# Attention taken head by head: projections between the scores, row sums in fours, norms in packs of four

## The reference

```python
x = x + 0.5 * ffn(layernorm(x))                  # gelu, 1024 -> 4096 -> 1024, weights changed per sequence
xn = x1 / max(|x1|, 1e-12) * sqrt(1024) * gamma  # x1 = layernorm(x)
q, k, v = split(xn @ w_qkv.T)                    # 8 heads of 128
sim = (q * 128 ** -0.5) @ k.T                    # causal mask, per head
out = softmax(sim) @ v                           # 2048 x 2048 per head
x = x + out @ w_out.T
x = x + 0.5 * ffn(layernorm(x))
```

## Time and profile before

| | us |
|---|---|
| median of 3 runs | 2884.86 |
| lowest of them | 2884.67 |
| profiled execution | 2884.55 |
| its span on the slowest core (core 3) | 2883.0 |
| spans of all cores | 2873.4 to 2883.0 |
| PE busy | 2762.4 (96%) |
| DVE busy | 1535.2 (53%) |
| ACT busy | 1173.1 (41%) |
| first attention, first projection to first output projection | 524.4 to 926.5 |

### The profile page before, as it was taken

One profiled execution on the slowest core, in us unless ns is written; L12 is line 12 of the kernel. 1 busy time (PEld: TensorE's weight loads), 2 busy tenths in 40 slices (PEclk: granted clock), 3 DMA queues, 4 the chain that ended last, 5 costly groups with the idle time before them and its releaser, 6 DMA issues.

```text
span 2883.0 us, 39821 instructions; the slowest of 8 cores (2873.4 to 2883.0 us)
## 1 busy us (share of the span) xinstructions
PE 2762.4 (96%) x12944; PEld 1259.0 (44%) x12944; DVE 1535.2 (53%) x2060; ACT 1173.1 (41%) x1901; POOL 34.5 (1%) x61
## 2 busy tenths in 40 slices
PE   4999999999999999999999999999999899999999
PEld 1444444444444444444444444444444443444444
DVE  6457447546346744744753663565452557456343
ACT  3331332468677233233223223226775852321320
POOL 0000000000000000000000000000000000000000
PEclk9999999999999999999999999999999999999999
DMA  5634433220020144653574354350301103446433
GB/s 164 219 118 145 165 124 129 37 45 1 1 59 1 59 159 138 214 190 139 192 224 147 114 157 155 116 111 7 45 1 23 37 1 112 151 151 200 147 132 132
DMA packets 57905, 321.55 MB, mean 112 GB/s; under 512 B 6384, under 2 KB 6512, under 8 KB 24944
## 3 DMA queue, kind: packets, MB, share of 16 engines
q1 hardware_dynamic: 43504, 281.26, 29.2%
q0 software_dynamic: 14208, 37.75, 6.4%
HBM read 318.99 MB, written 16.78 MB: 116 GB/s over the span
## 4 chain that ended last, share of the span: by engine, by line
PE 92%; DVE 4%; issue 2%; DMA 1%; ACT 1%; SPq 0%; DVEq 0%; ACTq 0%
PE ps L392 31%; PE ps L376 29%; PE ps L432 7%; PE ps L477 4%; PE ps L469 4%; PE ps L435 4%; PE ps L457 4%; PE ps L491 4%; PE ps L334 1%; PE ps L311 1%; DVE tB L852 1%; DVE wb L751 1%; PE ps L444 1%; PE ps L301 1%; DMA xn<-wall 1%
## 5 line engine op out<-in xcount | busy, mean ns | idle before, releaser
L751 DVE SCALAR_TENSOR_TENSOR wb<-ps,oddc,xn 128x512 bf16<-128x512 f32 x1024 | 692.0, 743 | 489.5 <-PE ps L334 439.2
L376 PE MATMUL ps<-xn,wb 128*128 128x512 bf16 x4096 | 911.6, 383 | 25.9 <-DVE xn L729 14.0
L392 PE MATMUL ps<-arena,wb 128*128 128x512 bf16 x4096 | 907.3, 379 | 0.0
L376 PEld LDWEIGHTS ps<-xn,wb 128*128 128x128 bf16 x4096 | 403.5, 99 | 526.0 <-issue 55.6
L392 PEld LDWEIGHTS ps<-arena,wb 128*128 128x128 bf16 x4096 | 401.2, 98 | 498.6 <-issue 24.1
L591 ACT ACTIVATE arena<-ps,small 128x512 bf16<-128x512 f32 x512 | 351.8, 687 | 575.8 <-PE ps L376 575.7
L665 ACT ACTIVATE pb<-ps,negm 128x512 bf16<-128x512 f32 (+3 forms) x640 | 353.5, 637 | 57.1 <-PE ps L460 31.8
L599 ACT ACTIVATE pb<-ps,b2half 128x512 f32<-128x512 f32 x128 | 88.0, 687 | 662.2 <-PE ps L392 662.2
L799 DVE TENSOR_TENSOR R<-R,pb 128x512 f32<-128x512 f32 x128 | 88.6, 692 | 378.6 <-ACT pb L599 378.4
L469 PE MATMUL ps<-pb,onesb 128*128 128x512 bf16 (+3 forms) x640 | 224.4, 356 | 29.9 <-DVE tB L852 17.2
L432 PE MATMUL ps<-xn,wb 128*128 128x512 bf16 x1024 | 237.9, 379 | 0.0
(11 more groups left out here) (61 smaller groups left out, 1307.1 us busy)
## 6 DMA issues: line engine op xcount, KB each, us to landing
xn<-wall SPq DMA_DIRECT2D x256, 1024.0 KB, 5.9
wb<-wall POOLq DMA_DIRECT2D x16, 1024.0 KB, 10.6
outT<-R POOLq DMA_DIRECT2D x24, 512.0 KB, 4.7
R<-xT SPq DMA_DIRECT2D x16, 512.0 KB, 9.0
R<-xT POOLq DMA_DIRECT2D x16, 512.0 KB, 7.4
outT<-R SPq DMA_DIRECT2D x16, 256.0 KB, 6.0
meanf<-mean_f SPq DMA_DIRECT2D x1, 64.0 KB, 8.9
meanb<-mean_bf SPq DMA_DIRECT2D x1, 32.0 KB, 9.5
```

The costliest lines, as they stand in the source:

```text
L376: m = pe.matmul(ps[i][:, :], wt[:, cc * 512 + i * 128: cc * 512 + (i + 1) * 128], xsl(st, cc, t0 + nh * 512), start=(cc == 0), stop=(cc == ...
L392: m = pe.matmul(ps[b][:, :], wt[:, k * 128:(k + 1) * 128], h_act(k // 4 + 8 * (k % 4), nh), start=(k == 0), stop=(k == HC - 1))
L751: i = dve.scalar_tensor_tensor(wb[n % 3][:, cc * 512:(cc + 1) * 512], ps[4][:, :], odd[:, i0 * 8 + cc: i0 * 8 + cc + 1], F[half][:, k * 51 ...
```

## The change

- One list, `SCHED`, holds the whole attention of a sequence. `FIRST` projects heads 0 and 1 of Q and K and the V of heads 0 to 3 ahead of the scores. The other 64 groups (`LATER`) are taken in half groups, eight matmuls each, between the score tiles: after each product with V as many as the rate gives, one half group for two tiles (128 half groups over the first 256 of 320 tiles). They and the norms use banks 6 and 7 by turns.
- A group of V now gives 256 tokens by two heads: two times eight matmuls of 256 columns. V is evicted by DVE, Q and K still by ACT.
- Scores use three banks (0, 1, 2), outputs banks 3 and 4 by turns, the row sums bank 5 alone. The sums of four tiles run in a row after the fourth product with V (`sum`); pb has eight slots.
- The norms of one head's four blocks of Q (or K) are made by four matmuls in a row, each against 32 columns of ones, each writing its own 32 partitions of one bank, followed by one maximum on DVE over the bank. `bound` joins the four maxima by a mask and one f32 matmul of 8 columns; `root` takes the square root by Ln and Exp; `shift` writes the head's own column of negm. For heads 0 and 1 the four squares of Q (K) are made after the fourth block, for the others after each block.
- The sums, squares, mean and variance of the norm of block 1024, and the sum of block 1536, go from the attention into the last two W2 groups of f1. The squares of block 1536 are taken by PE before groups 1 to 4 of the attention and made by ACT after groups 0 to 3.
- The slabs of attention are loaded in the order V, Q, K. K is held for three heads, V for four, in a ring.

The diff, cut to its core (PE's part, then ACT's, then DVE's; the old loops that the new ones replace are printed above):

```diff
-KT0, V0, QT0 = 0, HPH * S, 2 * HPH * S
+QO0, K0, V0, NSQ0 = 0, HEADS * S, HEADS * S + 3 * S, HEADS * S + 3 * S + 4 * S
...
-PROJ = []
-for _nbs in ((0, 1), (2,), (3,)):
-    for _kind in ("q", "k"):
-        for _h in range(HPH):
-            for _nb in _nbs:
-                PROJ.append((_kind, _h, _nb))
...
...
+FIRST = [("q", h, nb) for h in range(2) for nb in range(2)] + [("v", p, t) for p in range(2) for t in range(4)]
+FIRST += [("k", h, nb) for h in range(2) for nb in range(2)]
+FIRST += [("q", 0, 2), ("q", 1, 2), ("v", 0, 4), ("v", 0, 5), ("v", 1, 4), ("v", 1, 5), ("k", 0, 2), ("k", 1, 2)]
+FIRST += [("q", 0, 3), ("k", 0, 3), ("v", 0, 6), ("v", 0, 7), ("v", 1, 6), ("v", 1, 7), ("q", 1, 3), ("k", 1, 3)]
+LATER = []
+for _h in range(2, HEADS):
+    _kinds = [("q", _h, nb) for nb in range(4)], [("k", _h, nb) for nb in range(4)]
+    if _h in (4, 6):
+        LATER += _kinds[0] if _h == 4 else []
+        LATER += [("v", _h // 2, t) for t in range(4)]
+        LATER += _kinds[1] if _h == 4 else _kinds[0] + _kinds[1]
+        LATER += [("v", _h // 2, t) for t in range(4, 8)]
+    else:
+        LATER += _kinds[0] + _kinds[1]
+def with_norms(groups, waiting):
+    out = []
+    for kind, h, nb in groups:
+        for half in range(2):
+            out.append(("proj", kind, h, nb, half))
+            for item in [i for n, i in waiting if n == 0]:
+                out.append(item)
+            waiting[:] = [(n - 1, i) for n, i in waiting if n > 0]
+        if kind == "v":
+            continue
+        if h >= 2:
+            out.append(("sq", kind, h, nb))
+        elif nb == 3:
+            out.extend(("sq", kind, h, i) for i in range(4))
+        if nb == 3:
+            waiting.append((1, ("norm", kind, h)))
+            if kind == "k":
+                waiting.extend([(3, ("bound", h)), (5, ("root", h)), (7, ("shift", h))])
+    return out
+def attn_schedule():
+    waiting = []
+    sched = with_norms(FIRST, waiting)
+    later = with_norms(LATER, waiting)
+    later += [i for n, i in waiting]
+    cost = [1 if i[0] == "proj" else 0 for i in later]
+    total, core = sum(cost), 0
+    done, pending, pre, g = 0, [], {}, 0
...
+        for st in steps:
+            sched.append(st)
+            if st[0] == "pv":
+                if st[3] % 4 == 3:
+                    sched.append(("sum", st[1], st[2], st[3] // 4, st[4], ui))
+                core += 1
+                while later and done <= total * core / (RATE * 40):
+                    item = later.pop(0)
+                    done += item[0] == "proj"
+                    sched.append(item)
+    assert not later
+    return sched
+RATE = 6.4
+SCHED = attn_schedule()
+S_BANK = (0, 1, 2)
+SUM_OF = {i[4]: (i[5], i[3] // 4) for i in SCHED if i[0] == "pv"}
+LAST_G = {i[5]: i[4] for i in SCHED if i[0] == "pv"}
...
-        pb = sb("pb", [128, 2048], BF16)
+        pb = sb("pb", [128, 4096], BF16)
...
+                if n == 15 and st == "f1" and ti == 1:
+                    ln_square("at", seq, 1024, 2 * t)
+                    ln_square("at", seq, 1024, 2 * t + 1)
+                    if t == 3:
+                        ln_mean("at", seq, 1024)
...
+                    if what == "proj" or what == "norm" or what == "bound":
+                        rot = (6, 7) if scoring else (0, 1, 2)
+                        b = rot[turn % len(rot)]
+                    if what == "proj":
+                        _, kind, h, nb, half = item
+                        if half == 0:
+                            if 1 <= groups < 5:
+                                ln_square("at", seq, 1536, 2 * (groups - 1))
+                                ln_square("at", seq, 1536, 2 * (groups - 1) + 1)
+                            if groups == 5:
                                 ln_mean("at", seq, 1536)
+                            groups += 1
+                            bank_free(b)
+                            wt = attn_slab(pe, ("at", seq, h // (2 if kind == "v" else 4), "qkv".index(kind)))
+                            pe.wait_ge(g["xnd"].sem,
+                                       g["xnd"].at(("at", seq, (nb // 2 if kind == "v" else nb) * 512, CC - 1)))
+                        if kind == "v":
+                            for cc in range(CC):
+                                m = pe.matmul(ps[b][:, half * 256:(half + 1) * 256],
+                                              xsl("at", cc, nb * 256 + half * 128, 128),
+                                              wt[:, cc * 512 + (h % 2) * 256: cc * 512 + (h % 2 + 1) * 256],
+                                              start=(cc == 0), stop=(cc == CC - 1))
+                        else:
+                            for cc in range(4 * half, 4 * half + 4):
+                                c0 = cc * 512 + (h % 4) * 128
+                                m = pe.matmul(ps[b][:, :], wt[:, c0:c0 + 128], xsl("at", cc, nb * 512),
+                                              start=(cc == 0), stop=(cc == CC - 1))
+                        if half == 1:
+                            m.then_inc(g["proj_mm"].sem, g["proj_mm"].up((seq, kind, h, nb)))
+                            freed[b] = ("v_ev" if kind == "v" else "proj_ev", (seq, kind, h, nb))
+                            turn += 1
+                    elif what == "norm":
+                        _, kind, h = item
                         bank_free(b)
+                        pe.wait_ge(g["nsq"].sem, g["nsq"].at((seq, kind, h, 3)))
+                        for j in range(4):
+                            m = pe.matmul(ps[b][32 * j:32 * j + 32, :], onesb[:, 0:32],
+                                          arena[:, NSQ0 + j * 512: NSQ0 + (j + 1) * 512], start=True, stop=True)
+                        m.then_inc(g["nrm_mm"].sem, g["nrm_mm"].up((seq, kind, h)))
+                        freed[b] = ("nmax", (seq, kind, h))
+                        turn += 1
+                    elif what == "bound":
+                        h = item[1]
+                        bank_free(b)
+                        pe.wait_ge(g["nmask"].sem, g["nmask"].at((seq, "k", h)))
+                        pe.matmul(ps[b][:, 0:8], meanf[:, :], nrd[:, :], start=True, stop=True).then_inc(
+                            g["bnd_mm"].sem, g["bnd_mm"].up((seq, h)))
+                        freed[b] = ("nprod", (seq, h, 0))
+                        turn += 1
...
+                        b = S_BANK[gi % 3]
+                        bank_free(b)
...
+                        ob, p0 = 3 + ui % 2, (gi % 8) * 512
...
+                    elif what == "sum":
+                        _, h, qb, batch, gi, ui = item
+                        if batch == 0:
+                            bank_free(5)
+                        for j in range(4):
+                            kt = 4 * batch + j
+                            w0 = 128 * max(0, kt - 4 * qb)
+                            p0 = ((gi - 3 + j) % 8) * 512
+                            m = pe.matmul(ps[5][:, w0:512], onesb[:, :], pb[:, p0 + w0:p0 + 512], start=(kt == 0),
+                                          stop=(kt == 4 * qb + 3))
+                        m.then_inc(g["rs_mm"].sem, g["rs_mm"].up((seq, ui, batch)))
+                        freed[5] = ("recip", (seq, ui))
...
+                        if n == 14 and a[0] == "at":
+                            ln_squares("at", seq, 1024)
+                        if n == 15 and a[0] == "at":
+                            ln_musq("at", seq, 1024)
+                            ln_rstd("at", seq, 1024)
...
+                        if groups < 4:
+                            ln_squares("at", seq, 1536, 2 * groups, 2 * groups + 2)
+                        if groups == 6:
+                            ln_musq("at", seq, 1536)
+                        if groups == 9:
+                            ln_rstd("at", seq, 1536)
+                        groups += 1
+                    elif what == "sq":
+                        _, kind, h, nb = item
+                        act.wait_ge(g["proj_ev"].sem, g["proj_ev"].at((seq, kind, h, nb)))
+                        if nb == 0 and held.get("nsq"):
+                            act.wait_ge(g["nrm_mm"].sem, g["nrm_mm"].at(held["nsq"]))
+                        c0 = qcol(h, nb) if kind == "q" else kcol(h, nb * 512)
+                        act.activation(arena[:, NSQ0 + nb * 512: NSQ0 + (nb + 1) * 512], arena[:, c0:c0 + 512],
+                                       AF.Square).then_inc(g["nsq"].sem, g["nsq"].up((seq, kind, h, nb)))
+                        if nb == 3:
+                            held["nsq"] = (seq, kind, h)
...
+                    elif what == "root":
+                        h = item[1]
+                        act.wait_ge(g["nprod"].sem, g["nprod"].at((seq, h, 1)))
+                        act.activation(nrx[:, 3:4], nrx[:, 2:3], AF.Ln, scale=float(DM * DM), bias=cols[:, 1:2]).then_inc(
...
+                        act.activation(nrx[:, 3:4], nrx[:, 3:4], AF.Exp, scale=0.5).then_inc(
```

(59 more changed lines are left out.)

306 lines of the change are left out of this document (115 added, 191 removed).

## The result

The changed kernel takes **2929.57 us** (median of its runs, lowest 2928.05), the kernel before 2884.86 (lowest 2884.67). The ratio is 1.015, with an interval of 1.012 to 1.018: about 45 us slower, under the 2% line. The profiled execution took 2929.54 us with a span of 2928.0, against 2884.55 and 2883.0. The forecast was +60, just over the 2% line; the sign was right and the range held the result, but the size was missed by 15 us.

What follows compares the result with a forecast made beforehand. PE, busy 96%, was taken as the bound. Waits and slow clock of 69.4 us per attention against 35 gave +69, norms -13, bounds and V +4.5: +60 on 2884.55, 2945 us; range 2892 to 2985.

Steps and rivals of the forecast that it cites:

- part 5: Slow clock per attention: seven half-clock stretches, 1.7 us each, four in the scores; 12 us, bounds 5 and 20.
- DVE terms: Between a unit's last sums and its reciprocal: norms 5.6 us, V evictions, bounds and shifts; 8.1 us per attention.
- score banks: In the scores, three banks instead of four: exponentials 0.1 us late after narrow scores, some 16 times; 1.5 us per attention.
- part 4: In the scores: DVE work ahead of the reciprocal 8.1 us, head 7 3.0, three score banks 1.5, per attention.
- head 7's bound and masks: At head 7, PE waits for the square and DVE's mask, and the exponentials for the root; 3.0 us per attention.
- Part 1: Seam from the first feed-forward: PE waits on squares, 1.1 us in W2, 7.8, and 5.5 over three groups; 14.4 per attention.
- Part 2: End of the first projections: PE waits for squares of heads 0 and 1 and the first exponential; 6.8 us per attention.
- Part 3: Row sums in bank 5 alone: waits on reciprocals, 12.6 us while projections last and 11.0 after, per attention.
- the 60 that the prediction gave as a sign of being right: Row-sum matmuls, all in bank 5, were to wait on reciprocals for 60 us or more in sum.
- below 94%: Whole kernel: PE's busy share was to fall below 94%, as a sign that the forecast was right.
- The first rival of the prediction: While projections last, other work covers the row sums' wait at each unit's first batch; 2898 us; chance 0.18.
- Part 6: Norms in 32 packs of four matmuls at 0.45 us each: 13 us won, range -20 to +11.

Runs made afterwards that it cites:

- e10: Changed kernel with block 1024's variance ahead of block 1536's adds, and PE taking 1536's squares two groups later; undisturbed cores 2896.1 to 2898.3 us.
- e5: Changed kernel with row-sum copy before the reciprocal, the seam's other order, and ACT instead of DVE evicting V; lowest 2853.53 us, ratio to before 0.990.
- e4: Changed kernel plus eight 512-column matmuls ahead of the first row sums of each attention's last five units; undisturbed cores 2919.8 to 2923.3 us.
- e8: Kernel before the change, with DVE copying the row sums out of their bank ahead of the reciprocal; lowest 2904.84 us, ratio to before 1.007.
- e11: Changed kernel with only DVE's copy of the row sums out of bank 5 ahead of the reciprocal; undisturbed cores 4 to 7 2895.4 to 2905.1 us.
- e3: Changed kernel with both the row-sum copy ahead of the reciprocal and the seam's other order; lowest 2880.11 us, ratio to before 0.992.

## Why the prediction missed the size, and what in it was right

The places of the waits and the sign were right; the size was 15 us too high, which put the forecast over the 2% line (0.48 was given to that side) and the result under it. The step that failed is part 5, the clock: it put 12 us of slow clock into each attention where there were 6.6, and so forecast 3.5 us more than before where none were added. Smaller shares of the miss are the DVE terms and the score banks of part 4. For each attention the length is set against the prediction's own count of issue, 368.4, less 6.9 for the packs and 2.6 for what moved into W2, plus 2.2 for bounds and V's halves: 361.1. The lengths of the two attentions on core 0, 419.6 and 426.0 us, leave 58.5 and 64.9 of gaps and slow clock, 61.7 in the mean, and 62.9 with the excess of the wait in W2 (1.2). The forecast had 69.4. By steps, means of both attentions:

| step | forecast | measured |
|---|---|---|
| 1 seam | 14.4 | 14.4 |
| 2 end of the first projections | 6.8 | 6.8 |
| 3, 4 row sums, and DVE work ahead of the reciprocal | 31.7 | 29.2 |
| 4 head 7's bound and masks | 3.0 | 1.9 |
| 4 three banks for scores | 1.5 | 0 seen |
| 5 clock | 12 | 6.6 |
| other gaps, most under 0.3 us | none | 4.0 |

- **Part 1 was right** in every link: 7.47 on the square against 7.8 with the second square, three waits of 1.36 against 1.8 less the 0.43 that always pass, 0.83 in W2 against 1.1. e10 took them away and got their time back.
- **Part 2 was right**: 3.7 on norms (L514) and 3.1 on the first exponentials, table loads 16 as said.
- **Part 3 was right** in its place and kind: all waits in bank 5, 0.2 to 0.6 in most units with projections, 1.85 to 2.25 without. As the profile counts waits they sum to 40.9 us in both attentions, not to the 60 that the prediction gave as a sign of being right (the table counts from issue to issue and takes in V's half groups, 58). PE busy came out at 94.5% and not below 94%. The first rival of the prediction, a covered wait, would have had none while projections last.
- **Part 4 was mis-sized**, by about a third of its DVE terms (29.2 less part 3's 23.6 leaves 5.6 of 8.1): the 0.9 for a norm put before the tail was forecast six times in an attention and shows at three places (672.61, 850.20, 886.46); elsewhere the waits are 0.2 to 0.7, and part of the delay appears as V's half groups waiting for their bank (4.7 in both). Head 7's cluster is 1.9, and three score banks cost nothing that shows: of the 4.4 us of L541 3.5 are the first scores of the two attentions, which part 2 has, and 0.9 belong to head 7's cluster.
- **Part 5, the clock, was the step that failed.** Its price of 1.7 for a stretch over busy PE was right, its count and its places were not. It put seven stretches at half clock into each attention, four of them within the scores. The trace of core 0 has four stretches of 3.4 us in the first attention and eight in the second. At the seam and in part 2 there are three and seven; in the scores one each, in head 7, where four were forecast. What it also missed: a stretch that lies over a wait costs only half of the time that PE works in it. The 6.8 us at the seam and the stretch at 919 (length, then PE busy; PEclk is the eighth figure from the left):

```profile
533.30:540.10 6.80, 2.73 (x7) 0.92 (x8) 4.68 (x7) 2.87 (x5) 0.00 (x0) 0.50 0.24 44
...
919.00:922.40 3.40, 3.22 (x11) 1.47 (x12) 2.54 (x3) 1.19 (x2) 0.00 (x0) 0.51 0.00 0
```

Of the first, PE works in 2.73 us of 6.80, so half speed costs 1.4 and not 3.4. Of the second it works in 3.22 and loses 1.6, but 0.9 of that comes back: the next wait on the reciprocal is 0.88 (924.09), where the second attention, with full clock there, has 1.78. All twelve stretches have 28.7 us of PE work in them, so they cost 14.4; less 1.2 for waits that got shorter, that is the 6.6 of the table. Before, core 3 had four and six stretches in its two attentions, all in the scores, with 6.5 and 9.4 us of such cost, 8.0 in the mean where the prediction had 8.5. So the change lost eight of the ten in the scores and got ten at the seam and in part 2, and the clock costs no more than it did. The prediction also counted six stretches behind the twelve borders of heads in the trace before; there are five (683.1, 710.4, 2123.5, 2270.3 and 2321.5 us).

- **Part 6 was right**: 0.43 per pack, forecast 0.45. The Trainium skill, "TensorEngine Tiling (Array Packing)", Key Properties, lets tiles run side by side and drains TensorE where the tiling mode changes. The measured 0.43 lies between the 0.24 of the first rule alone and the 0.55 with two drains; against one untiled matmul's 0.216 the pack has 0.09 us more ahead of it and 0.12 more behind it. That fits a price at each change of mode, smaller than was modelled; no run separates it from another cost of the pack. (The 0.24 itself stands in no row: by the earlier trace rows one matmul's issue is 0.216.)

The table's difference of 6.5 per attention is 13 of the 15 us between 60 and 45, and the clock is the largest share of it. Of the other 2, one lies in the kernel before (402.1 and 405.6 us leave 33.7 and 37.2 of gaps and slow clock, 35.5 in the mean and not 35), the rest in the packs at 0.43 in place of 0.45. (The scores of the kernel before have 9.4 and 8.8 us without a matmul by the earlier trace rows, not 5 to 9; the sum does not use it.) That the total came within 15 us owes something to luck: the other steps had 10.5 us per attention too much, and 4.0 of small gaps, put at nothing, stood against it. Where these gaps come from, and some 4 of e5's 28, stays open.

## What to carry to other kernels

When two changes put the same bank into every unit, price the bank by the whole stay: from the last write to the end of the slowest reader (here 3.36 us of reciprocal plus 0.5), less the PE work that stands between (part 3, e4). An in-order engine that carries both the pacing operation and small evictions makes a wait that moves: free one resource, and PE stops at the next thing which that engine holds (e8, e11), so move work off the engine (e5) as well. Where squares, a root and evictions share one engine's order, put the variance that releases the root ahead of the long adds of the next block (e10).

## What was not expected of the hardware

- A reciprocal of 128x512 f32 took 3.36 us read from the bank and 3.35 from SBUF, where copy and multiply took 0.69: the source makes no difference, and it alone is seven tenths of the 4.7 us that a unit costs DVE in e11.
- Whether a wait brings the granted clock to 0.5 is not told by its length alone: the twelve waits of 2.9 or 3.0 us in e8 (core 4) and the four of 3.0 to 3.3 in before (core 3) each had a stretch at 0.5 within 1 us, the twelve of 1.5 us in before five between them. Four waits of 2.10 us before V's half groups each had a stretch within 1 us of them in e3 (core 4), the same waits of e11, at 705 and 791 us, had none, and the five waits of 0.88 to 2.25 us on row sums in the last five units of after had one between them. The two attentions of one execution, with the same instructions, had 13.7 and 27.3 us of it.
